# Two PSUM banks for scores used in turn, a new order of work where attention meets the dense feed-forward, and the centring of output rows moved within a batch

## The chip, the cores and the metric

The kernel runs on one NeuronCore of a Trainium2 chip. A core has a matrix engine (PE, with its weight loads shown as PEld), a vector engine (DVE), an activation engine (ACT), GpSimd (POOL) and an engine that issues DMAs (SP). Each runs its own list of instructions in order and waits for the others by semaphores. The metric is the time of one execution in microseconds (us) on the device.

## What is computed

Sixteen sequences of 128 tokens of width 128 go through two layers. All is float32.

```python
x = x + ffn0(attn0(x))     # multi-query attention, 16 heads of 64, relative bias, null key; then layernorm
                           # ffn0: layernorm, 128->512, gelu, layernorm, 512->128, ternary weights
x = x + moe1(attn1(x))     # attention with a given bias per sequence and head, then layernorm
                           # moe1: top 2 of 8 experts, 320 slots each, 128->512, relu, 512->128
# attention, for one sequence b:
xn = ln(x[b]);  q, k, v = xn @ Wq, xn @ Wk, xn @ Wv      # one k and v for all heads
sim = q @ k.T * scale + bias;  sim = where(causal & mask, sim, -big)
out = ln(softmax(sim) @ v @ Wo) * g_out
```

## The kernel before

One batch is one sequence. Both attention layers run a loop over 16 batches, written out for the first and last few and as a hardware loop for those between. The queries of a batch are cut into four units u of 32 query rows. A unit covers all 16 heads, and since attention is causal it needs `WIDTH[u]` = 33, 65, 97, 129 keys.

For each unit PE makes scores in the PSUM tile `psS`, which has two banks: one matmul for each half h of the heads (`scores`, L843 to L857). DVE adds bias and mask, takes the row maximum and writes `sc` (`biased`, L1543 to L1549, four instructions, each of which increments `scores_ready`). ACT takes the exponential (L1255). DVE divides (`divide`, the tile `pn`), PE transposes (`turn_pair`, `turn_probs`), ACT copies to `PT`, PE multiplies by the values (`values_pair` for units 0 and 1, `values` for units 2 and 3), DVE adds the null value and writes `OT` (`outputs`), and PE multiplies by the output weights (`project`). Before the change half h of every unit goes to bank h, so `scores` of unit n waits until `biased` of unit n-1 has ended (`scores_ready` at 4n).

In layer 2 the layernorm of the output rows is spread over later batches on DVE: `out_stats` and `moments`, `variance`, a power of -1/2 on POOL (`output_rstd`), `centre(b-3)` (L1605 to L1611, two instructions, at 128x8 and 128x128, which read two operands from SBUF) and `rescale(b-3)` (L1615). In the kernel before `centre` stands in unit 0 of batch b, behind `divide(B-1, 3)` and ahead of `input_norm(1, b+2)` (tile `xn`, L1498), and `rescale` in unit 1. POOL adds bias and mask for the next batch (`mask_bias`, L630, four instructions each batch) once `output_rstd` is done.

The dense feed-forward stands between the layers. Its 16 tiles are four quads g. PE transposes a quad (`f_turn`), multiplies up (`f_up`, four blocks j), ACT takes the gelu and squares (`f_gelu`, `f_square`), POOL sums squares (`f_squares`), PE multiplies down (`f_down`, 16 tiles), DVE reads the sums and updates the rows X (`f_read`, `f_update`) and takes the statistics of the new rows (`f_input_stats`), whose power POOL takes (`f_input_rstd`). The first seam is where layer 1 ends: the last `values` and `project` on PE, then `f_turn(0)`, `f_up(0, 0)`, `down_sums` and `gate_fold`. The second is where layer 2 begins: `turn_input(1, 0, 0)` needs `xn` of batch 0, then `project_in(0, 0)`, the last four `f_down`, and the first scores.

## Time and profile before

| | us |
|---|---|
| median of 3 runs | 612.4 (610.82 to 613.22) |
| the profiled execution | 614.04 |
| its span, first to last instruction | 612.3 |

The program is bound by no engine all the way: over the span PE is busy 80%, DVE 71%, ACT 62%, POOL 51%. The mean granted clock of PE is 0.931 of full speed. In the page's 40 slices (15.3 us each) PE is at 9 tenths in most of layer 1 (from about 50 to 215 us), at 7 to 9 in the feed-forward and layer 2 (to about 469 us), at 4, 1 and 9 in the routing and the start of the experts. A view's idle time stands in brackets or behind a bar, with the instruction that ended it. Where an engine is late, the chain of waits that ended last passes through it.

### The profile page before, as it was taken

Reading aid. Unit: us, or ns where it says so; the run is one execution under the profiler, and the core shown is the slowest. Engines: PE = TensorE matmul, PEld = TensorE weight load, DVE = VectorE, ACT = ScalarE, POOL = GpSimd, SP = SyncE. Lnnn points to the kernel's source line nnn. Section 1 sums busy time; section 2 is a strip of 40 time slices with the busy share of each in tenths; the row PEclk is TensorE's granted clock in tenths of the full one; section 3 lists DMA queues with packets and bytes.
Section 4 is the critical chain, followed back from the end, with each engine's and each line's share of the span. In section 5 each row is a group of like instructions: output and inputs, shape, how many; then the busy total and the mean of one; then the engine's idle time right before and its main releaser. Section 6 shows DMA issues by size and latency. Waiting matters only on the chain.

```text
span 612.3 us, 13755 instructions
## 1 busy us (share of the span) xinstructions
PE 491.3 (80%) x3220; PEld 395.2 (65%) x3220; DVE 433.2 (71%) x2148; ACT 377.9 (62%) x1475; POOL 310.9 (51%) x368
## 2 busy tenths in 40 slices
PE   3678999999999877948898998988978419999920
PEld 1456777777777655647787887867756307878720
DVE  4899999999999775554778898899797603343403
ACT  1677898888888655634878778767775003443510
POOL 4576666655656517664433343344755531545560
PEclk9789999999999899978899999999998758999975
DMA  5450028331000000000021120000101021222117
GB/s 171 104 151 19 21 60 140 90 97 54 6 8 6 6 1 1 1 0 8 5 77 40 42 75 4 8 6 10 40 26 36 33 74 31 70 61 74 42 34 210
DMA packets 54696, 29.73 MB, mean 49 GB/s; under 512 B 19884, under 2 KB 51572, under 8 KB 54644
## 3 DMA queue, kind: packets, MB, share of 16 engines
q1 hardware_dynamic: 48900, 22.09, 14.6%
q0 software_dynamic: 2560, 4.90, 2.5%
q10 hardware_dynamic: 3184, 2.16, 1.1%
q8 instruction: 18, 0.29, 0.2%
q14 instruction: 34, 0.28, 0.2%
HBM read 16.13 MB, written 10.90 MB: 44 GB/s over the span
## 4 chain that ended last, share of the span: by engine, by line
PE 45%; DVE 20%; issue 14%; POOL 7%; DMA 5%; ACT 4%; SPq 1%; DVEq 1%; another core or an unknown queue 1%; ACTq 0%; POOLq 0%
PE psS L855 9%; PE psS L1152 5%; DVE sc L1547 5%; PE psA L910 4%; PE psO L891 4%; PE psQ L828 4%; PE psQ L812 3%; PE psQ L1142 3%; PE psT L873 2%; DVE centred L1610 2%; DVE OT L1571 2%; POOL wide_buf L630 2%; PE psA L1142 1%; PE psO L1142 1%; ACT qT L1238 1%
## 5 line engine op out<-in xcount | busy, mean ns | idle before, releaser
L1255 ACT ACTIVATE sc<-sc,negmax 128x97 f32<-128x97 f32 (+3 forms) x512 | 179.0, 354 | 34.0 <-DVE negmax L1547 32.2
L855 PE MATMUL psS<-kk,qT 128*128 128x194 f32 (+3 forms) x512 | 104.7, 327 | 23.9 <-DVE negmax L1547 22.2
L1547 DVE CUSTOM_DVE_ANT_0 sc<-psS,wide_buf 128x97 f32<-128x97 f32 (+3 forms) x512 | 93.6, 238 | 29.6 <-PE psS L855 26.6
L630 POOL TENSOR_TENSOR wide_buf<-bias,mask 128x132 f32<-128x132 f32 (+3 forms) x128 | 109.5, 881 | 9.8 <-DVE negmax L1547 4.2
L855 PEld LDWEIGHTS psS<-kk,qT 128*128 128x128 f32 x512 | 79.0, 195 | 50.3 <-issue 47.5
L1255 ACT ACTIVATION_READ_ACCUMULATOR sc<-sc,negmax 128x1 f32 x512 | 97.4, 190 | 0.0
L577 POOL TENSOR_TENSOR qrn<-qssc,half 128x9 f32<-128x9 f32 (+1 forms) x32 | 55.8, 1745 | 59.1 <-DVE qssc L1533 59.1
L1559 DVE TENSOR_TENSOR pn<-sc,rsum 128x128 f32<-128x128 f32 (+3 forms) x128 | 71.7, 560 | 6.8 <-DVE rsum L1555 0.2
L910 PE MATMUL psA<-Wo,OT 128*128 128x128 f32 (+1 forms) x512 | 65.2, 281 | 1.7 <-DVE OT L1571 1.7
L910 PEld LDWEIGHTS psA<-Wo,OT 128*128 128x128 f32 x512 | 62.1, 195 | 2.5 <-DVE OT L1571 2.5
L1571 DVE TENSOR_SCALAR OT<-psO,cols 128x512 f32<-128x512 f32 x64 | 47.6, 744 | 2.7 <-PE psO L891 1.8
L1268 ACT COPY PT<-psT 96x512 f32<-96x512 f32 x64 | 37.0, 577 | 15.8 <-PE psT L873 9.9
L873 PE MATMUL psT<-ident,pn 128*96 128x128 f32 (+1 forms) x256 | 39.6, 278 | 6.0 <-issue 4.1
L1547 DVE DVE_READ_ACCUMULATOR2_ANT negmax<- 128x1 f32 x512 | 41.6, 81 | 0.4 <-issue 0.2
L748 POOL DMA_INDIRECT choice_rows<-hT,tags x24 | 22.5, 939 | 37.1 <-ACT hT L1398 24.5
L891 PE MATMUL psO<-PT,vp 96*64 96x256 f32 (+1 forms) x256 | 34.8, 390 | 7.9 <-DVE OT L1571 4.3
L873 PEld LDWEIGHTS psT<-ident,pn 128*96 128x96 f32 (+1 forms) x256 | 28.5, 137 | 19.1 <-issue 18.5
L642 POOL DMA_INDIRECT slot_rows<-Y,dest_u x32 | 31.4, 980 | 18.1 <-issue 6.7
L812 PE MATMUL psQ<-Wq,xnT 128*128 128x512 f32 x64 | 36.7, 660 | 1.1
L1238 ACT ACTIVATE qT<-psQ 128x512 f32<-128x512 f32 x64 | 34.6, 586 | 4.5 <-PE psQ L841 4.1
L613 POOL TENSOR_TENSOR vp<-kvs,vnull 128x64 f32<-128x64 f32 x32 | 12.9, 403 | 47.2 <-PE psO L891 47.1
L828 PE MATMUL psQ<-xnT,Wq 128*128 128x128 f32 x256 | 32.9, 284 | 0.0
(298 smaller groups left out, 1004.1 us busy)
## 6 DMA issues: line engine op xcount, KB each, us to landing
slot_rows<-empty SPq DMA_DIRECT2D x2, 1390.0 KB, 9.7
xb<-slot_rows SPq DMA_DIRECT2D x16, 139.0 KB
vp_u<-vp SPq DMA_DIRECT2D x128, 8.0 KB, 1.7
choice_rows<-zero_row SPq DMA_DIRECT2D x8, 256.0 KB, 3.0
wide_buf<-choice_rows SPq DMA_DIRECT2D x8, 256.0 KB, 4.7
vp_u<-vp SPq DMA_DIRECT2D x64, 16.0 KB, 1.8
eW<-in_L_ffn_W SPq DMA_DIRECT2D x4, 256.0 KB, 3.0
gT<-in_L_ffn_W SPq DMA_DIRECT2D x4, 256.0 KB, 3.2
```

What stands on the lines that cost most here:

```text
L577: pool.tensor_tensor(dst, src, half[:, 0:k], ALU.pow).then_inc(done, count)
L630: pool.tensor_tensor(unit_masked(i, u).rearrange("p h e k -> p (h e) k"), unit_bias(layer, u).rearrange("p h e k -> p (h e) k"), mask[laye ...
L812: pe.matmul(psQ[:, h, :], xnT[i][:], Wq[0][:, 512 * h:512 * (h + 1)], start=True, stop=True).then_inc(s["q_psum"], 1)
L828: m = pe.matmul(psQ[:, h, j * P:(j + 1) * P], Wq[1][:, (4 * h + j) * P:(4 * h + j + 1) * P], xnT[i][:], start=True, stop=True)
L855: m = pe.matmul(psS[:, h, 0:2 * w], qT[i][:, h, u].rearrange("p m q -> p (m q)"), kk[i][:, :, 0:w], start=True, stop=True)
L873: m = pe.transpose(psT[0:k, probs_bank(u, i), g * P:(g + 1) * P], pn[u][:, g, :], ident[:])
L891: m = pe.matmul(psO[DH * e:DH * (e + 1), 2 * P * (u - 2):2 * P * (u - 1)], vp[i][0:k, :], PT[u - 1][0:k, :, e, :], start=True, stop=True)
L910: m = pe.matmul(psA[:, Y_AT[layer]:4 * P], OT[i][:, j].rearrange("p u q -> p (u q)"), Wo[layer][:, j, :], start=(j == 0), stop=(j == 7))
L1255: m = act.activation(v, v, ACT.Exp, bias=negmax[:, u, g:g + 1], scale=-1.0, accum_out=psum_row[:, u, g:g + 1])
L1547: dve.tensor_tensor_reduce(sc[u][:, h, e, :], unit_psum(u)[:, h, e, :], unit_masked(i, u)[:, h, e, :], -1.0, -FAR, ALU.add, ALU.min, accum ...
L1559: dve.tensor_tensor(pn[u][:], sc[u][:].rearrange("p h e k -> p (h e) k")[:, :, 1:k + 1], rsum[:, u, :].unsqueeze(2).broadcast_to([P, 4, k] ...
L1571: dve.tensor_scalar(OT[i][:, :, 2 * half_of:2 * half_of + 2, :], v, cols[:, C_VN:C_VN + 1], None, ALU.add).then_inc(s["out_ready"], 1)
```

## The change

It has three parts.

1. `score_bank`: unit 0 and 2 have both halves in bank 0, unit 1 in bank 1. Unit 3, which is too wide for one bank, puts half 0 in bank 1 and half 1 in bank 0. `scores` of unit 1, 2 and half 0 of unit 3 wait only for the unit before the last, and half 1 of unit 3 waits for unit 2. Unit 0 waits as before.
2. The seams. On PE `f_turn(0)` is moved ahead of the last `values`, `f_up(0, 0)` ahead of the last `project`, and the wait for the last gelu behind the transposition for layer 2. On DVE `null_keys` and the two `input_norm` of layer 2 are moved from behind `f_input_stats(2)` to ahead of `f_read(2)`, and `values_in(1, 0, 0)` to behind `f_read(2)`. On POOL `f_input_rstd(2)` is moved behind `mask_bias` and `values_set` of layer 2's batch 0.
3. `centre(b-3)` is moved from unit 0 to unit 2 and `rescale(b-3)` from unit 1 to unit 3.

```diff
+        def score_bank(u, h):
+            w = WIDTH[u]
+            if u == UNITS - 1:
+                return psS[:, 1 - h, 0:2 * w]
+            return psS[:, u % 2, 2 * w * h:2 * w * (h + 1)]
...
-                      (s["scores_ready"], 4 * n))
+                      (s["scores_ready"], 4 * (n - u) if u < 2 else 4 * (n - 1)))
                 for h in range(2):
-                    m = pe.matmul(psS[:, h, 0:2 * w], qT[i][:, h, u].rearrange("p m q -> p (m q)"),
+                    if u == UNITS - 1 and h == 1:
+                        apart(pe, (s["scores_ready"], 4 * n))
+                    m = pe.matmul(score_bank(u, h), qT[i][:, h, u].rearrange("p m q -> p (m q)"),
...
                 if g:
                     f_scale(g - 1)
+                if g and g < QUADS - 1:
                     f_input_rstd(g - 1)
...
             values_set(1, 0, 0)
+            f_input_rstd(QUADS - 2)
             f_scale(QUADS - 1)
...
-            pe.wait_ge(s["f_gelu"], 4 * QUADS)
             pe.wait_ge(s["y_done"], NB)
             turn_input(1, 0, 0)
+            pe.wait_ge(s["f_gelu"], 4 * QUADS)
             project_in(0, 0)
...
-                        if u == 0 and normed_now:
-                            centre(b - 3, 1 - i)
                         if u == 0 and not last and not no(b, NB - 2):
                             input_norm(1, b + 2, i)
+                        if u == 2 and normed_now:
+                            centre(b - 3, 1 - i)
...
-                        if u == 1 and normed_now:
+                        if u == 3 and normed_now:
                             rescale(b - 3, 1 - i)
```

PE at the first seam, before: the last transposition of probabilities (L873), the last `values` (L891) and `project` (L910), then `f_turn(0)` (L1070), `f_up(0, 0)` (L1076) and the two lines of `down_sums`.

```order
L873 MATMUL psT<-ident,pn 128x128 x4
L891 MATMUL psO<-PT,vp 64x256 x4
L910 MATMUL psA<-Wo,OT 128x128 x8
L1070 MATMUL psT<-ident,z 128x128 x4
L1076 MATMUL psQ<-hT,w1T 128x512
L1056 MATMUL psO<-w2g,ones 128x128 x4
L1058 MATMUL psO<-w2T,cols 128x128 x4
```

The same place after; lines of the changed kernel are 6 to 11 higher.

```order
L881 MATMUL psT<-ident,pn 128x128 x4
L1076 MATMUL psT<-ident,z 128x128 x4
L899 MATMUL psO<-PT,vp 64x256 x4
L1082 MATMUL psQ<-hT,w1T 128x512
L918 MATMUL psA<-Wo,OT 128x128 x8
L1062 MATMUL psO<-w2g,ones 128x128 x4
L1064 MATMUL psO<-w2T,cols 128x128 x4
```

The transposition and the first up-product have moved in between `values` and `project`, and `down_sums` now follows `project` directly.

DVE at the second seam, before: the end of `f_read(2)`, then `f_update(2)`, `f_input_stats(2)`, the null keys, `xn` and `kvs` (`values_in`).

```order
L1918 SCALAR_TENSOR_TENSOR zve<-fst,fms 128x4
L1923 TENSOR_SCALAR zs<-zrstd,nwm 128x4
L1926 SCALAR_TENSOR_TENSOR X<-ffo,zs,X 128x128 x4
L1933 BN_STATS stats<-X 128x6 x4
L1936 BN_AGGR mv<-stats 128x2 x4
L1938 TENSOR_SCALAR ve<-mv 128x4
L1455 COPY kk<-cols 64x1 x4
L1498 TENSOR_SCALAR xn<-X,mv,rstd 128x128 x2
L1513 COPY kvs<-psA 128x64
```

The same place after, from the end of `f_input_stats(1)`.

```order
L1949 TENSOR_SCALAR ve<-mv 128x4
L1465 COPY kk<-cols 64x1 x4
L1508 TENSOR_SCALAR xn<-X,mv,rstd 128x128 x2
L1925 COPY fst<-psS 128x2
...
L1929 SCALAR_TENSOR_TENSOR zve<-fst,fms 128x4
L1523 COPY kvs<-psA 128x64
L1934 TENSOR_SCALAR zs<-zrstd,nwm 128x4
L1937 SCALAR_TENSOR_TENSOR X<-ffo,zs,X 128x128 x4
```

`xn` now stands ahead of the reads of quad 2, and `kvs` behind them.

DVE in layer 2's loop, unit 0 to 1, before: `pn` of the last batch's unit 3, the two instructions of `centre`, `xn`, and the first of `biased` of unit 1 (rows named ISA without a tile are waits).

```order
L1559 TENSOR_TENSOR pn<-sc,rsum 128x512
L1607 REGISTER_ALU
L1608 ISA
L1608 SCALAR_TENSOR_TENSOR centred<-gate_sum,o_mv,Y 128x8
L1610 ISA
L1610 SCALAR_TENSOR_TENSOR centred<-Y,o_mv,g_out 128x128
L1498 ISA x2
L1498 TENSOR_SCALAR xn<-X,mv,rstd 128x128
L351 ISA
L1547 ISA sc,negmax<-psS,wide_buf 128x65
```

The same place after, and the new place of `centre` in unit 2.

```order
L1570 TENSOR_TENSOR pn<-sc,rsum 128x512
L1508 ISA x2
L1508 TENSOR_SCALAR xn<-X,mv,rstd 128x128
L355 ISA
L1557 ISA sc,negmax<-psS,wide_buf 128x65
...
L1608 BN_AGGR o_mv<-o_st 128x2
L1619 ISA
L1619 SCALAR_TENSOR_TENSOR centred<-gate_sum,o_mv,Y 128x8
L1621 ISA
L1621 SCALAR_TENSOR_TENSOR centred<-Y,o_mv,g_out 128x128
L355 REGISTER_ALU
L1557 ISA sc,negmax<-psS,wide_buf 128x129
```

`xn` now follows `pn` directly, and `centre` stands ahead of `biased` of unit 3. ACT's order is the same in both kernels.

## Rows read from the trace of the kernel before

**Rows 1.** Windows: stretch, length; busy PE, PEld, DVE, ACT, POOL; granted clock; DMA.

```profile
322.37:390.77 68.40, 62.41 (x469) 54.50 (x469) 58.78 (x306) 54.75 (x241) 26.33 (x36) 1.00 0.14 37
390.77:468.90 78.13, 66.67 (x483) 56.19 (x484) 68.28 (x384) 56.59 (x253) 38.54 (x48) 0.98 0.07 20
468.90:504.77 35.87, 11.40 (x94) 9.53 (x91) 15.20 (x80) 4.29 (x15) 17.40 (x20) 0.70 0.19 54
```

**Rows 2.** Groups of PE, layer 1, 50:214.9: count, busy, mean ns, idle before.

```profile
L855 PE MATMUL psS<-kk,qT 128*128 128x66 f32 (+3 forms) x224 | 45.1, 323 | 4.6 <-DVE negmax L1547 3.0
```

**Rows 3.** Groups of PE, six steady batches of layer 2, 322.3:390.7.

```profile
L855 PE MATMUL psS<-kk,qT 128*128 128x194 f32 (+3 forms) x96 | 18.9, 318 | 2.0 <-DVE negmax L1547 2.0
...
L891 PE MATMUL psO<-PT,vp 96*64 96x256 f32 (+1 forms) x48 | 6.5, 388 | 2.4 <-DVE OT L1571 2.4
```

**Rows 4.** Groups of PE, the last batches of layer 2, 390.77:468.9.

```profile
L855 PE MATMUL psS<-kk,qT 128*128 128x194 f32 (+3 forms) x104 | 21.4, 328 | 7.7 <-DVE negmax L1547 7.6
...
L891 PE MATMUL psO<-PT,vp 96*64 96x256 f32 (+1 forms) x56 | 7.6, 389 | 1.6 <-DVE OT L1571 1.6
```

**Rows 5.** Timeline of DVE in one steady batch: start, us, instruction.

```profile
341.21 0.95 DVE L1559 TENSOR_TENSOR pn<-sc,rsum 128x512 f32<-128x512 f32 x1
342.09 0.86 DVE L1608 SCALAR_TENSOR_TENSOR centred<-gate_sum,o_mv,Y 128x8 f32<-128x8 f32 x1
342.87 1.30 DVE L1610 SCALAR_TENSOR_TENSOR centred<-Y,o_mv,g_out 128x128 f32<-128x128 f32 x1
344.09 0.34 DVE L1498 TENSOR_SCALAR xn<-X,mv,rstd 128x128 f32 x1
```

**Rows 6.** Timeline of POOL, the same batch.

```profile
340.56 3.46 POOL L630 TENSOR_TENSOR wide_buf<-bias,mask 128x132 f32<-128x132 f32 x4
```

**Rows 7.** Timeline of PE, the same batch; in brackets the idle time before it.

```profile
345.15 0.90 PE L855 MATMUL psS<-kk,qT 128*128 128x194 f32 x4 [0.40 <-DVE negmax L1547]
```

**Rows 8.** Groups of DVE, `centre` behind layer 2's loop, 470:490.

```profile
L1610 DVE SCALAR_TENSOR_TENSOR centred<-Y,o_mv,g_out 128x128 f32<-128x128 f32 x3 | 1.0, 345 | 0.0
...
L1608 DVE SCALAR_TENSOR_TENSOR centred<-gate_sum,o_mv,Y 128x8 f32<-128x8 f32 x3 | 0.7, 224 | 2.9 <-POOL o_rs L577 2.9
```

**Rows 9.** Groups of DVE, five steady batches, 339:396.7, widest and narrowest `biased`.

```profile
L1547 DVE CUSTOM_DVE_ANT_0 sc<-psS,wide_buf 128x129 f32<-128x129 f32 x20 | 4.6, 288 | 3.6 <-PE psS L855 3.6
...
L1547 DVE CUSTOM_DVE_ANT_0 sc<-psS,wide_buf 128x33 f32<-128x33 f32 x20 | 2.8, 193 | 2.4 <-PE psS L855 2.4
```

**Rows 10.** Timeline of DVE, batch 0 of layer 2.

```profile
286.74 1.25 DVE L1498 TENSOR_SCALAR xn<-X,mv,rstd 128x128 f32<-128x128 f32 x1
```

**Rows 11.** Timeline of PE at the first seam.

```profile
222.81 1.09 PE L891 MATMUL psO<-PT,vp 96*64 96x256 f32 x8 [0.88 <-issue]
224.74 2.05 PE L910 MATMUL psA<-Wo,OT 128*128 128x128 f32 x16 [0.85 <-DVE OT L1571]
...
228.10 1.13 PE L1076 MATMUL psQ<-hT,w1T 128*128 128x512 f32 x2 [0.87 <-ACT hT L1351]
229.06 1.05 PE L1056 MATMUL psO<-w2g,ones 128*128 128x128 f32 x8
```

**Rows 12.** Timeline of PE at the second seam.

```profile
273.13 0.44 PE L801 MATMUL psA<-ident,xn 128*128 128x128 f32 x1 [7.21 <-issue]
...
275.05 3.48 PE L828 MATMUL psQ<-xnT,Wq 128*128 128x128 f32 x16
...
278.48 1.06 PE L1085 MATMUL psS<-w2g,gT 128*128 128x129 f32 x8
...
282.86 0.41 PE L819 MATMUL psA<-Wkv,xnT 128*128 128x64 f32 x2
...
283.39 1.95 PE L828 MATMUL psQ<-xnT,Wq 128*128 128x128 f32 x16
285.18 0.56 PE L855 MATMUL psS<-kk,qT 128*128 128x66 f32 x4
```

**Rows 13.** Timeline of POOL at the second seam.

```profile
273.01 3.00 POOL L630 TENSOR_TENSOR wide_buf<-bias,mask 128x132 f32<-128x132 f32 x4
```

More of the change, by code:

```diff
@@ L989, in attention_first @@
                 turn_probs(NB - 1, 3, 1)
-                values(NB - 1, 1)
-                project(0, NB - 1, 1, False)
             def attention_second():
@@ L1089, in f_down @@
                           stop=True).then_inc(s["f_o_psum"], 1)
+            pe.wait_ge(s["probsT_ready"], 3 * NB - 1)
+            f_turn(0)
+            values(NB - 1, 1)
             pe.wait_ge(s["g_WoT"], 2)
-            pe.wait_ge(s["probsT_ready"], 3 * NB)
-            f_turn(0)
+            f_up(0, 0)
+            project(0, NB - 1, 1, False)
             for g in range(QUADS):
                 for j in range(FB):
-                    f_up(g, j)
+                    if g or j:
+                        f_up(g, j)
                     if g == 0 and j == 0:
@@ L1546, in biased @@
                     h, e = g // 2, g % 2
-                    dve.tensor_tensor_reduce(sc[u][:, h, e, :], unit_psum(u)[:, h, e, :], unit_masked(i, u)[:, h, e, :],
+                    dve.tensor_tensor_reduce(sc[u][:, h, e, :], score_bank(u, h)[:, e * WIDTH[u]:(e + 1) * WIDTH[u]],
+                                             unit_masked(i, u)[:, h, e, :],
                                              -1.0, -FAR, ALU.add, ALU.min,
@@ L1942, in _ @@
                     f_norm_in(g + 2)
+                if g == QUADS - 2:
+                    null_keys(cols[:, C_NK:C_NK + 1])
+                    dve.wait_ge(s["x_rstd"], 1)
+                    input_norm(1, 0, 0)
+                    input_norm(1, 1, 1)
                 f_read(g)
+                if g == QUADS - 2:
+                    values_in(1, 0, 0)
                 f_update(g)
                 f_input_stats(g)
-            null_keys(cols[:, C_NK:C_NK + 1])
-            dve.wait_ge(s["x_rstd"], 1)
-            input_norm(1, 0, 0)
-            input_norm(1, 1, 1)
-            values_in(1, 0, 0)
             f_read(QUADS - 1)
-            dve.wait_ge(s["x_rstd"], QUADS - 1)
+            dve.wait_ge(s["x_rstd"], QUADS - 2)
             attention_second()
```

2 lines of the change are left out of this document (removed).

## Prediction

> **What bounds the kernel now.** I read the stretches first, then what PE waits for in each, then single batches. The windows show that PE is nearly full in the steady part of layer 2, 62.4 of 68.4 us, with 6.0 us idle in six batches, and less full in its last batches, 66.7 of 78.1 [rows 1]. So in attention a gain is at most PE's idle time. The groups of PE say who ends that idle time. In layer 1 the scores matmuls have 4.6 us of idle ahead of them from 50 to 215 us, about 14 batches [rows 2]. In the six steady batches of layer 2 it is 2.0 us ahead of scores and 2.4 ahead of `values`, both ended by DVE [rows 3], and in the last batches 7.7 and 1.6 [rows 4]. At the seams PE idles for another reason: it stands at one instruction whose operand comes late while later work would be ready. The largest such hole is 7.21 us, ahead of layer 2's first transposition [rows 12].
>
> Why DVE is late in layer 2 is seen in one batch. `pn` of unit 3 takes 0.95 us, then the two instructions of `centre` take 0.86 and 1.30, and `xn` 0.34 [rows 5]. The same two take 0.22 and 0.35 behind the loop [rows 8]. In the loop they run while POOL's four adds run, from 340.56 to 344.02 [rows 6], and the second ends just behind the last add. So (0.86 - 0.22) + (1.30 - 0.35) = 1.6 us of each batch is DVE standing behind POOL. It makes `biased` of unit 1 late, for which PE's scores of unit 2 wait 0.40 [rows 7], and then `OT`, for which `values` waits 2.4 / 6 = 0.40 [rows 3].
>
> **Part 1 and 3 in layer 2.** With alternating banks the scores of unit 2 wait for unit 0, which has long been read, so their 0.40 goes whether DVE is faster or not. With `centre` gone from unit 0, `xn` is next behind `pn`, and POOL's adds still run. An `xn` that starts under POOL's adds is held too: in batch 0 it took 1.25 us in place of 0.34 [rows 5, 10]. So the stall is not removed whole. `centre`'s first instruction shows what one such wait costs there, 0.64, since it was let in when POOL's third add ended. I give `xn` that wait and drop the second one, so DVE reaches unit 1 some 1.2 us earlier, at 343.1 in place of 344.3. Then `pn` of unit 0 may stand behind the fourth add until 344.1. `OT` still ends about 1.0 us sooner, and PE, which comes 0.4 sooner, finds it. So of the 0.73 us per batch ahead of scores and `values` nearly all goes: 4.2 us in six batches, and 0.7 in the batch before them, which is built alike. What comes late next is the transposition of unit 3 behind `pn`, which the change does not touch; it is part of the 6.0 - 4.4 = 1.6 us of idle that stay.
>
> The moved instructions cost at their new places 0.22 + 0.35 in unit 2 and 0.28 in unit 3. In the steady batches DVE waits there for PE: in five batches 3.6 us ahead of the widest `biased` (unit 3) and 2.4 ahead of the narrowest (unit 0), 0.7 and 0.5 a batch [rows 9], and POOL's adds are over by then. Behind them stand `biased` of unit 3 and of unit 0. I cost both at nothing; without that cover they would be 0.3 us a batch, some 3 us in all.
>
> In the last batches DVE has the routing too and is itself the bound. The bounds for these 78 us are what six steady batches give, 4.4, and all idle ahead of scores and `values`, 9.3 [rows 4]. Unit 0's scores keep their old wait, and part of the 7.7 is theirs. But each stall taken from DVE counts there in full. I take 6.0. Layer 2 sums to 4.2 + 0.7 + 6.0 = 10.9 us, bounds 3 and 14.
>
> The Trainium skill, SBUF — State Buffer, section "Who interferes with whom", says that a DVE instruction with two SBUF inputs, or a one-input `tensor_scalar` in a two-port mode, shares its second port with GpSimd, and that whoever starts first holds it for a whole instruction. It speaks against part 3 so far as `xn` is a `tensor_scalar` and inherits the place; with the rule taken as one add per wait the sum is as above, and with `xn` missing the gap between two adds it is rival A. The trace agrees that `xn` can be held, 1.25 against 0.34 us.
>
> **Part 1 in layer 1.** Of the 4.6 us ahead of scores 3.0 are waits long enough to be given to DVE, and 1.6 are short ones [rows 2]. Half 0 of unit 3 no longer waits for unit 2, and half 1, which does, has half 0's own matmuls ahead of it as cover. The larger waits are DVE being late as a whole, and a bank more lets PE run ahead by one unit. Bounds 0 and 4.6; I take 2.0, the short ones and a little. The added wait in unit 3 has behind it all of PE, but it is for what the old one waited for.
>
> **The first seam.** PE waits 0.88 for `values`, 0.85 for `project` and 0.87 for `f_up(0, 0)`, the last for ACT's copy of `hT` [rows 11]. Now the four transpositions of `f_turn(0)` run in the first hole, and ACT's copy runs under `values` (1.09). `f_up(0, 0)` takes 229.06 - 228.10 = 1.0 and fills the second hole. `values` ends at 222.81 + 1.09 = 223.9 as before, `f_up` at 224.95, which is when `project` starts in place of 224.74, and with its 2.05 us `down_sums` starts at 227.0 in place of 229.06 [rows 11]. Everything behind it waits for it: DVE's `c2`, POOL's adds to X, and the fold of the gate. That is 2.1 us; bounds 1 (if POOL's and DVE's work behind it holds part back) and 2.5.
>
> **The second seam.** PE ended its last ready work at 273.13 - 7.21 = 265.92 [rows 12]. The `xn` of batches 0 and 1 are rows of quad 0, final long before, so DVE can write them ahead of `f_read(2)`. That puts six short instructions ahead of reads, of which the last waits for PE's work that ends at 265.92 anyway, so they cost nothing. From there: the transposition, ACT's copy and the first matmuls of `project_in`, 275.05 - 273.13 = 1.9 at the low clock, for which I take 1.4; the sixteen of L828, 1.95; the four `f_down`, 282.86 - 278.48 = 4.4; `project_in` of batch 1, 285.18 - 282.86 = 2.3; in all 10.05 us [rows 12]. The first scores come at 276.0 in place of 285.18: 9.2 us. The clock: the hole was followed by 3.48 us for sixteen matmuls that take 1.95 otherwise [rows 12], the 1.2 GHz level in place of 2.4. Without the hole I take the high level; if it drops all the same, 2 us are lost.
>
> Two things stand against it. POOL now does `mask_bias` of batch 0 some 4 us earlier, beside DVE's `f_update(2)`, four instructions with two SBUF operands each. They may be held for most of POOL's 3.00 us of adds [rows 13], which puts `f_read(3)`'s end about where PE comes to the first scores. And POOL's power of quad 2 now stands ahead of `f_scale(3)`, so the adds for batch 1 start about 1 us later against the first scores than before. Bounds 4 and 11, value 9.2, since PE's own work is nearest to the end.
>
> **Sum.** 10.9 + 2.0 + 2.1 + 9.2 = 24.2 us. The profiled execution took 614.04, which gives 589.8. The median of the runs shown is 1.6 lower, so **588.2**. Routing and experts (from 469 us on) are unchanged in order and shift as a whole.
>
> **Rivals.** A: *`xn` takes over the stall.* If `xn` always waits for POOL's last add, as in batch 0 (1.25 us) [rows 10], DVE's chain is shorter only by 0.3 us. The scores of unit 2 go early, but `values` waits for the same `OT`; layer 2 gives 3 and the time is 596. For it speaks that row, against it that `pn` and the first `centre` instruction each got in between two adds [rows 5]. B: *the second seam gives half.* POOL's order or the low clock holds the first batch back: 4 to 5 us less, 593. For it speaks that batches 0 and 1 depend on DVE, POOL and PE at once; against it PE's count above [rows 12]. C, *slower:* PE is granted 1.2 GHz in attention. The change moves idle time, and layer 2 at the low level would run near 1.8 times as long for its 62.4 us of PE work in 68.4 [rows 1]. It costs 0.45 us for each us spent there, so it outweighs 24 us from a spell of some 55 us on, and 3 us more make it slower: 616. Against it: the clock is 1.00 in that stretch, and even behind layer 2, where PE is busy 11.4 of 35.9 us, the mean is 0.70, some 21 us at the low level [rows 1]. D: *the waits are only renamed*, the bound in attention being a loop through DVE and ACT: only the seams gain, 601. Against it is that PE is 91% busy in the steady batches.
>
> **How the numbers follow.** The forecast has 0.68, A 0.12, B 0.12, D 0.03, C 0.02, and 0.03 is left for something that cancels all. The terms' own bounds give 582 to 594 for the forecast's case. The range of 582 to 598 takes in A and B. A measurement of this kernel tells about 0.5% (3 us) from no change. Faster by more holds in the forecast, A, B and D: 0.95; within 0.5% 0.03; slower 0.02.
>
> **What would show it.** After the change PE's groups should show under 1 us ahead of scores and under 0.5 ahead of `values` in six steady batches, and a batch should take 10.6 us in place of 11.4. `xn` in unit 0 should take about 1 us, `centre` 0.22 and 0.35. The first scores of layer 2 should start some 13 us earlier, near 272, and layer 1 end 2 us earlier. `xn` at 1.3 us in every batch with `OT` still ending PE's idle would be A; a hole of 4 us or more around the first scores would be B; a clock under 0.9 in layer 2 would be C. The prediction is wrong as a whole if a batch of layer 2 still takes 11.2 us.

## The result, and the profile after the change

The changed kernel takes 587.8 us (median of 4 runs, 587.1 to 592.0); the kernel before, run beside it, 611.6. The ratio is 0.962, 95% interval 0.958 to 0.966. Two later sets of runs of the same kernel gave 588.5 and 588.3 us, with ratios of 0.962 and 0.961. The forecast was 588.2.

The profiled executions differ by more, 612.3 and 586.0, 26.3 us. The table splits them by what can be read in a timeline of PE: the start of the first scores matmul of a batch. "Again" is the same changed kernel in the profiles of the two later sets.

| stretch (us) | before | after | again | again |
|---|---|---|---|---|
| layer 1, batch 2 to 15 | 154.1 | 152.9 | 152.9 | 152.9 |
| batch 15 to layer 2's first scores (both seams) | 79.1 | 67.2 | 66.2 | 66.3 |
| layer 2, batches 0 to 2 | 31.9 | 32.7 | 33.4 | 33.7 |
| layer 2, batches 3 to 9 | 79.7 | 73.1 | 73.1 | 73.1 |
| layer 2, batches 10 to 14 | 61.2 | 56.6 | 57.7 | 57.3 |
| batch 15 to the end | 154.3 | 151.9 | 151.3 | 151.7 |

The seam's 67.2 and 66.2 differ by a spell at the lower level of the clock (granted 0.50, 1.2 GHz). In the first profile of the changed kernel it lies from 205.0 to 208.4, at the end of layer 1, and PE is busy throughout it; the other two have none there. The kernel before has one at the same place, from 206.6 to 210.0, so its 79.1 is best set against 67.2.

Of the last row's 2.4 to 3.0 us, 1.7 to 2.1 lie behind the last matmul, where nothing was changed. That tail is 26.4 us in the profile of before, 24.3 to 24.7 in the three of the changed kernel and 23.3 to 24.4 in the four that carry one part each. So some 2 us of the 26.3 belong to the tail of the one profile that there is of the kernel before, which fits that the medians differ by less than the spans.

The groups of PE's instructions in the changed kernel say where the idle time went. Columns: line, operation, tiles, count, busy us, mean ns, idle us just before. First layer 1, 50:213, then the steady batches of layer 2, 309:377, then the last ones, 377.5:444. They answer to [rows 2], [rows 3] and [rows 4]. The line ahead of them is the kernel before, layer 1, 50:215.

```profile
L873 PE MATMUL psT<-ident,pn 128*96 128x128 f32 (+1 forms) x112 | 17.5, 280 | 1.4 <-issue 0.3
```

```profile
L863 PE MATMUL psS<-kk,qT 128*128 128x66 f32 (+3 forms) x224 | 45.1, 323 | 1.6 <-DVE negmax L1557 1.6
...
L881 PE MATMUL psT<-ident,pn 128*96 128x128 f32 (+1 forms) x112 | 17.5, 280 | 3.3 <-issue 3.1
```

```profile
L863 PE MATMUL psS<-kk,qT 128*128 128x194 f32 (+3 forms) x104 | 20.0, 314 | 0.0
L899 PE MATMUL psO<-PT,vp 96*64 96x256 f32 (+1 forms) x56 | 7.6, 392 | 0.0
L881 PE MATMUL psT<-ident,pn 128*96 128x128 f32 (+1 forms) x48 | 7.4, 276 | 2.1 <-issue 1.9
```

```profile
L863 PE MATMUL psS<-kk,qT 128*128 128x66 f32 (+3 forms) x95 | 18.6, 315 | 2.6 <-DVE negmax L1557 2.6
...
L899 PE MATMUL psO<-PT,vp 96*64 96x256 f32 (+1 forms) x48 | 6.5, 390 | 1.9 <-DVE OT L1582 1.9
```

In the steady batches the idle time ahead of scores (2.0) and of `values` (2.4) is gone. What is left stands ahead of the transposition of unit 3. In layer 1 the 4.6 us ahead of scores became 1.6, but the group of transpositions, 1.4 before, now has 3.3: of the 3.0 us that are gone in one place 1.9 stand in another.

The windows of the changed kernel, for [rows 1]: length, busy PE, PEld, DVE, ACT, POOL, granted clock, share of DMA. One steady batch has no idle time of PE at all, and batch 0 has a great deal.

```profile
304.45:314.58 10.13, 10.13 (x81) 8.91 (x80) 8.77 (x52) 9.04 (x40) 4.50 (x6) 1.00 0.21 60
304.40:377.40 73.00, 70.88 (x548) 62.31 (x548) 63.32 (x356) 63.26 (x281) 31.99 (x42) 1.00 0.16 43
```

The same for batch 0, the changed kernel and then the kernel before:

```profile
271.71:284.26 12.55, 7.83 (x43) 6.83 (x41) 9.00 (x58) 9.79 (x41) 8.04 (x10) 0.73 0.05 10
```

```profile
285.18:296.90 11.72, 8.42 (x43) 7.19 (x41) 8.80 (x54) 8.85 (x39) 6.87 (x9) 0.71 0.03 7
```

DVE in one steady batch, for [rows 5], and POOL there, for [rows 6] (start, duration, instruction), then the groups of DVE in five such batches, 325:377.4:

```profile
347.47 0.86 DVE L1570 TENSOR_TENSOR pn<-sc,rsum 128x512 f32<-128x512 f32 x1
348.25 0.92 DVE L1508 TENSOR_SCALAR xn<-X,mv,rstd 128x128 f32 x1
...
346.74 3.44 POOL L634 TENSOR_TENSOR wide_buf<-bias,mask 128x132 f32<-128x132 f32 x4
```

```profile
L1508 DVE TENSOR_SCALAR xn<-X,mv,rstd 128x128 f32 x5 | 4.8, 967 | 0.0
...
L1621 DVE SCALAR_TENSOR_TENSOR centred<-Y,o_mv,g_out 128x128 f32<-128x128 f32 x5 | 1.7, 341 | 0.0
...
L1619 DVE SCALAR_TENSOR_TENSOR centred<-gate_sum,o_mv,Y 128x8 f32<-128x8 f32 x5 | 1.0, 195 | 0.0
```

`centre` takes 0.20 and 0.34 at its new place, where POOL is idle, and `xn` has inherited the held place: 0.97 in place of 0.34.

PE's timelines at the two seams answer to [rows 11] and [rows 12]:

```profile
221.19 1.09 PE L899 MATMUL psO<-PT,vp 96*64 96x256 f32 x8 [0.44 <-issue]
222.21 1.12 PE L1082 MATMUL psQ<-hT,w1T 128*128 128x512 f32 x2
223.17 2.00 PE L918 MATMUL psA<-Wo,OT 128*128 128x128 f32 x16
225.01 1.06 PE L1062 MATMUL psO<-w2g,ones 128*128 128x128 f32 x8
```

```profile
261.74 0.31 PE L807 MATMUL psA<-ident,xn 128*128 128x128 f32 x1
...
263.12 1.95 PE L834 MATMUL psQ<-xnT,Wq 128*128 128x128 f32 x16
...
271.71 0.56 PE L863 MATMUL psS<-kk,qT 128*128 128x66 f32 x4
```

From `values` to `down_sums` it was 6.25 us (222.81 to 229.06) and is 3.82. At the second seam the hole of 7.21 us is gone and the first scores start at 271.71. But behind them, in batch 0, there is a new one:

```profile
279.07 1.20 PE L863 MATMUL psS<-kk,qT 128*128 128x258 f32 x2 [3.99 <-DVE negmax L1557]
```

### The profile page after: what moved, and what is told of

The parts are those of the page before. It is cut to its first block, busy times and chain, and to the rows that moved or that the text cites. A ratio compares the mean times of both kernels' runs of the same rounds, so it can differ in the third digit from the quotient of the medians.

```text
span 586.0 us, 13781 instructions
## 1 busy us (share of the span) xinstructions
PE 483.6 (83%) x3220; PEld 390.9 (67%) x3220; DVE 426.4 (73%) x2148; ACT 377.5 (64%) x1475; POOL 312.0 (53%) x368
## 3 DMA queue, kind: packets, MB, share of 16 engines
q1 hardware_dynamic: 48900, 22.09, 15.1%
## 4 chain that ended last, share of the span: by engine, by line
PE 59%; DVE 12%; issue 11%; POOL 6%; ACT 4%; DMA 4%; SPq 1%; another core or an unknown queue 1%; DVEq 0%; ACTq 0%; POOLq 0%
PE psS L863 10%; PE psA L918 7%; PE psS L1162 5%; PE psQ L834 4%; PE psT L881 4%; PE psO L899 4%; PE psQ L818 4%; PE psQ L1152 3%; PE psO L889 2%; DVE sc L1557 2%; PE psO L890 2%; DMA slot_rows<-Y,dest_u 1%; ACT qT L1248 1%; PE psO L1152 1%; PE psA L1152 1%
## 5 line engine op out<-in xcount | busy, mean ns | idle before, releaser
L863 PE MATMUL psS<-kk,qT 128*128 128x194 f32 (+3 forms) x512 | 102.7, 322 | 11.6 <-DVE negmax L1557 11.6
L581 POOL TENSOR_TENSOR qrn<-qssc,half 128x9 f32<-128x9 f32 (+1 forms) x32 | 55.9, 1748 | 57.8 <-DVE qssc L1543 57.7
L881 PE MATMUL psT<-ident,pn 128*96 128x128 f32 (+1 forms) x256 | 39.6, 278 | 11.0 <-issue 10.6
L617 POOL TENSOR_TENSOR vp<-kvs,vnull 128x64 f32<-128x64 f32 x32 | 14.1, 440 | 40.3 <-PE psO L899 40.2
L1979 DVE TENSOR_SCALAR hm<-psQ,cols 128x320 f32<-128x320 f32 x16 | 8.8, 551 | 32.4 <-PE psQ L1152 32.4
```

The source lines that it names most:

```text
L581: pool.tensor_tensor(dst, src, half[:, 0:k], ALU.pow).then_inc(done, count)
L863: m = pe.matmul(score_bank(u, h), qT[i][:, h, u].rearrange("p m q -> p (m q)"), kk[i][:, :, 0:w], start=True, stop=True)
L881: m = pe.transpose(psT[0:k, probs_bank(u, i), g * P:(g + 1) * P], pn[u][:, g, :], ident[:])
```

## The experiments

### One part at a time

Four kernels, each the kernel before with one part of the change: alternating banks with the split of unit 3 (its two halves in different banks), the order at both seams, `centre` and `rescale` two units later, and the second seam alone. The first and the third edit are these; the seams are the pieces of the diff shown ahead of the prediction.

```
-                      (s["scores_ready"], 4 * n))
+                      (s["scores_ready"], 4 * (n - u) if u < 2 else 4 * (n - 1)))
...
+                    if u == UNITS - 1 and h == 1:
+                        apart(pe, (s["scores_ready"], 4 * n))
```

```
-                        if u == 0 and normed_now:
+                        if u == 2 and normed_now:
                             centre(b - 3, 1 - i)
...
-                        if u == 1 and normed_now:
+                        if u == 3 and normed_now:
                             rescale(b - 3, 1 - i)
```

Part 1 alone:

> The kernel before with part 1 alone (alternating banks). Theory: in layer 2 PE's idle time ahead of scores is only where DVE's lateness shows first, so with the bank free PE does the scores of unit 2 at once and then waits for the same OT ahead of values. Six steady batches stay at about 68 us, the idle ahead of scores falls from 2.0 to near 0 and that ahead of values rises from 2.4 to 4 or more; the gain is layer 1's, 2 to 3 us in all: 608.5 to 610. Rival: the shared banks cost PE in layer 2 as the rows say, 2.0 us in six batches and part of 7.7 in the last ones; then the gain is 7 to 9 us, 603 to 605.

Part 2 alone:

> The kernel before with part 2 alone (both seams). Theory: 2.1 us at the first seam and 9.2 at the second, of which about 1 is given back in layer 2's batch 0, where POOL's adds and DVE's update of quad 3 now stand closer to the first scores: 600.5 to 602. Rival: the seams only shift the point at which DVE and POOL are full, and part is lost again in the first batches: 604 or more.

Part 3 alone:

> The kernel before with part 3 alone (centring in unit 2). Theory: DVE's stall behind POOL's adds is what makes PE wait both ahead of scores and ahead of values, so this part alone gives nearly all of layer 2's gain: 9.5 to 12 us, 600 to 602; a steady batch takes 10.5 to 10.6 us in place of 11.4, xn about 0.9 us, centre 0.2 and 0.35. Rival: half of it needs the free bank: 4 to 6 us, 606 to 608.

The second seam alone:

> The kernel before with the second seam's order alone. Theory: the seams add up, the second gives 8 to 9.5 us, 602 to 603.5, and the first what is between this and both seams, about 2. Rival: PE's clock falls to 1.2 GHz behind the seam all the same or batch 0 waits longer, and the second seam gives 6 us or less, 605.5.

Measured, beside the kernel before at 611.7 us, with the stretches of the profiles:

| | banks | both seams | second seam | centring |
|---|---|---|---|---|
| median, us | 607.7 | 600.8 | 603.1 | 602.4 |
| ratio | 0.994 (0.991 to 0.997) | 0.985 (0.980 to 0.991) | 0.988 (0.983 to 0.994) | 0.987 (0.981 to 0.994) |
| layer 1, batch 2 to 15 | 152.9 | 154.0 | 154.0 | 154.1 |
| both seams | 77.9 | 66.2 | 68.6 | 79.0 |
| layer 2, batches 0 to 2 | 31.3 | 33.9 | 33.5 | 31.9 |
| batches 3 to 9 | 79.1 | 79.7 | 79.7 | 72.7 |
| batches 10 to 14 | 60.1 | 61.1 | 60.3 | 59.4 |

All four medians lie in the theory's ranges or within 1 us of them. The ratios' gains sum to 3.3%, 20.4 us with the two seams counted once, against 3.8% of the whole change; the intervals are wide enough for the parts to be additive.

The stretches are sharper than the medians, since most of them repeat to 0.1 us. The 6.6 us of layer 2's steady batches are wholly those of part 3: with it alone they take 72.7, with the banks alone 79.1, with both 73.1. The groups of PE in the steady batches show what the banks do there. First the banks alone (318.5:386.5), then the centring alone (321.5:383.5):

```profile
L861 PE MATMUL psS<-kk,qT 128*128 128x194 f32 (+3 forms) x98 | 18.7, 311 | 0.0
...
L897 PE MATMUL psO<-PT,vp 96*64 96x256 f32 (+1 forms) x48 | 6.5, 388 | 4.6 <-DVE OT L1578 4.6
```

```profile
L855 PE MATMUL psS<-kk,qT 128*128 128x194 f32 (+3 forms) x96 | 18.7, 316 | 0.0
...
L891 PE MATMUL psO<-PT,vp 96*64 96x256 f32 (+1 forms) x48 | 6.5, 392 | 0.0
```

With the banks alone the wait ahead of scores is gone, and the one ahead of `values`, 2.4 in [rows 3], is 4.6: PE reaches the same late `OT` earlier. With the centring alone both waits are gone, and no bank is needed. The seams are worth 79.1 - 66.2 = 12.9, of which 1.2 is not theirs: with the banks alone, which touch no seam, the same stretch is 77.9. Of this 1.0 is the clock and not the banks; the other 0.2 stand behind layer 2's first transposition and were not followed up. The profiles of the kernel before and of the centring alone have the spell at 1.2 GHz at the end of layer 1 (206.6 to 210.0 and 206.3 to 209.7), and from the first scores of batch 15 to the end of the last `values` both take 17.8 us. The profiles of the banks, of both seams and of the second seam have none there and take 16.8. Among these three the second seam gives 77.9 - 68.6 = 9.2 and the first 68.6 - 66.2 = 2.4. Both kernels with the new second seam then lose 1.6 to 2.0 us in batches 0 to 2.

### What in part 1 helps layer 1

The changed kernel with one change in a wait: the first half of unit 3 waits for unit 2 too, so the banks alternate but the split covers nothing.

```
-                      (s["scores_ready"], 4 * (n - u) if u < 2 else 4 * (n - 1)))
+                      (s["scores_ready"], 4 * (n - u) if u < 2 else (4 * (n - 1) if u == 2 else 4 * n)))
```

> The changed kernel, but in unit 3 the first half of the scores waits for unit 2 as the second half does. It prices the split inside part 1. My theory: of the 1.6 us that layer 1 gained most is the wait of unit 2, which now looks two units back, and little is the split: layer 1, from its first to its last batch, stays within 0.4 us of the changed kernel's (180.0 in its profile), the time within 1 us of it (587 to 589), and layer 2's steady batches stay at 10.4 us. Rival (the gain of layer 1 is the split, since its matmuls cover the wait of unit 3): layer 1 is 1 to 1.6 us longer and the time 589 to 590.

It took 591.1 us, ratio 0.966 (0.963 to 0.969). Layer 1 from batch 2 to 15 takes 154.1 us, what it took before the change; so here the rival was right and my theory wrong. The groups of PE in layer 1, 50:213:

```profile
L863 PE MATMUL psS<-kk,qT 128*128 128x66 f32 (+3 forms) x222 | 43.2, 315 | 3.4 <-DVE negmax L1557 1.8
...
L881 PE MATMUL psT<-ident,pn 128*96 128x128 f32 (+1 forms) x112 | 17.2, 276 | 4.5 <-issue 4.4
```

The alternation as such gives layer 1 nothing. The gain of 1.2 us there is the split, which gives PE half of unit 3's matmuls while it would wait. Layer 2's steady batches seem to lose by the split: 72.75 us without it, 73.05 with it, and 72.71 with no bank changed at all. But all of that is one batch, the sixth of the seven, which takes 11.06 us with the split and 10.32 without; the six others together are 0.4 us shorter with it. In that batch `pn` of unit 3 starts 0.1 us later against POOL's adds. DVE and POOL, first the changed kernel, then the one without the split:

```profile
357.96 1.43 DVE L1570 TENSOR_TENSOR pn<-sc,rsum 128x512 f32<-128x512 f32 x1
...
356.94 3.44 POOL L634 TENSOR_TENSOR wide_buf<-bias,mask 128x132 f32<-128x132 f32 x4
```

```profile
358.89 0.69 DVE L1570 TENSOR_TENSOR pn<-sc,rsum 128x512 f32<-128x512 f32 x1
...
357.96 3.46 POOL L634 TENSOR_TENSOR wide_buf<-bias,mask 128x132 f32<-128x132 f32 x4
```

It starts 1.02 us behind the first add in one and 0.93 in the other, and takes 0.74 us more; PE's stop ahead of the transposition that needs it is 0.93 us in place of 0.19. So this stall does cost time, unlike that of `xn`, which comes next.

### Whether the stall that `xn` took over costs time

```
-                        if u == 0 and not last and not no(b, NB - 2):
+                        if u == 1 and not last and not no(b, NB - 2):
                             input_norm(1, b + 2, i)
```

> The changed kernel, with input_norm (DVE's xn) moved from unit 0 of a batch to unit 1 in layer 2. My theory: in the changed kernel xn has inherited the place behind pn of unit 3 and is held there by POOL's adds (0.97 us for work of 0.34), but PE is full in the steady batches (idle 2.1 us in seven, all of it ahead of a transposition), so DVE's lost time costs nothing: the time stays within 1 us of the changed kernel's 587.8, the steady batch stays at 10.4 us, xn falls to 0.35 to 0.5 us, and what comes next behind pn (biased of unit 1) starts some 0.6 us earlier. Only in the last batches, where DVE has the routing too, up to 1 us may come. Rival (the inherited stall still costs, case A of the prediction): 3 to 5 us less, 583 to 585, with a steady batch of 10.1 us.

It took 589.5 us, ratio 0.961 (0.959 to 0.964); the changed kernel in the same set 588.5, 0.962. The group of DVE in five steady batches, 325:377.4, and the window of seven batches:

```profile
L1570 DVE TENSOR_TENSOR pn<-sc,rsum 128x128 f32<-128x128 f32 x5 | 4.0, 797 | 0.7
...
L1508 DVE TENSOR_SCALAR xn<-X,mv,rstd 128x128 f32 x5 | 1.7, 331 | 0.0
```

```profile
304.40:377.40 73.00, 70.88 (x549) 62.34 (x548) 61.87 (x357) 63.28 (x280) 31.99 (x42) 1.00 0.16 43
```

`xn` falls from 0.97 to 0.33 us, and the seven batches take 73.02 us in place of 73.05, with PE busy 70.88 us in the same 73.00 as before. The place of `xn` costs nothing there, as the theory has it. But the stall isn't gone: `pn` of unit 0, the next instruction with two operands in SBUF, now takes 0.80 us in place of 0.34, and DVE's busy time over the seven batches falls by 1.45 us only, 0.2 a batch. So the run shows that 0.2 us less of DVE and an earlier `biased` of unit 1 bring nothing; it doesn't show what a DVE without any stall would bring. That stalls still cost time is seen elsewhere: of PE's 2.1 us of idle time in these seven batches 1.8 stand ahead of the transposition of unit 3 in two batches, where `pn` of unit 3 was held to 1.13 and 1.43 us.

### The hole in batch 0

Two steps of DVE in batch 0 go one unit later each (the first edit); then that together with `xn` in unit 1; then an Exp of one column ahead of layer 2 (the second edit), alone and with the two others. The changed kernel ran beside them in both sets.

```
-                        if first and u == 1:
+                        if first and u == 2:
                             f_update(QUADS - 1)
-                        if first and u == 2:
+                        if first and u == 3:
                             f_input_stats(QUADS - 1)
```

```
             queries(1, 0, 0)
+            act.activation(warm[:], cols[:, C_GIN1:C_GIN1 + 1], ACT.Exp, scale=0.0)
             attention_second()
```

`f_update(3)` later:

> The changed kernel, with two steps of DVE in batch 0 of layer 2 each put one unit later: f_update(3) from unit 1 to unit 2, f_input_stats(3) from unit 2 to unit 3. My theory: PE's hole of 3.99 us ahead of the second half of unit 3's scores in that batch is made by DVE, whose biased of unit 2 stands behind f_update(3), 0.28 + 1.67 us; it starts 1.9 us earlier now and the hole becomes 2.0 to 2.2 us. Without a spell at 1.2 GHz behind it batch 0 takes 9.9 to 10.6 us in place of 12.55; with one it takes 10.6 to 11. The time is 1.5 to 2.7 us less than the changed kernel's, 585 to 586.3. Rival (the hole is the latency of the chain through ACT's exponentials when the pipeline fills, and f_update only stands in it): no change, 587 to 588, with the hole still over 3.3 us.

That and `xn` in unit 1:

> The changed kernel, with input_norm in unit 1 and f_update(3) and f_input_stats(3) of batch 0 each one unit later. My theory: the sum of the two runs before, which is the second one's alone: 585 to 586.3, first batch of layer 2 at 10 to 11 us. Rival: with xn in unit 1 of batch 0 that unit's chain becomes longer again by 0.4 us, and 0.4 us of the gain goes.

The changed kernel beside them:

> The changed kernel itself, beside its variants on the same chip. Every theory expects 587 to 588.5 us and, in its profile, 12 to 13 us for batch 0 of layer 2 with a hole of 3 to 4 us ahead of the second half of unit 3's scores. If the spell at 1.2 GHz in that batch is an accident of this one trace, it is absent here.

The early Exp:

> The changed kernel, with one more instruction of ACT: an Exp of one column into a tile that nobody reads, behind queries(1, 0, 0), ahead of layer 2. There ACT is idle for 5.8 us, and in batch 0 its first exponential is preceded by a table load of 1.28 us. My theory: batch 0 is a chain that fills (scores, biased, exponentials, divide, next scores), and PE's hole in it is the length of that chain, of which the table load is 1.28 us; f_update(3) only stands in it behind. With the load done early the first exponentials start 1.3 us sooner and the hole of 3.99 us becomes 2.7 to 3.0; batch 0 is 1.0 to 1.3 us shorter, and the time 586 to 587.3. Rival (POOL's adds then hold f_update(3) by as much, or the hole is DVE's own work): under 0.4 us in batch 0, no change.

All three edits:

> The kernel with input_norm in unit 1 and f_update(3) and f_input_stats(3) one unit later (e7), with the early Exp too. My theory: e7's hole of 2.23 us in batch 0 is the wait for the first exponentials and falls to about 1.0; batch 0 takes 10.0 to 10.4 us in place of 11.5, and the time is 1.0 to 1.3 us under e7's, 3 to 3.5 under the changed kernel's: 584 to 585.5. Rival (the clock falls to its lower level in batch 0 all the same and stretches PE's own work there): batch 0 stays over 10.8 us and half of the gain goes.

The changed kernel beside these:

> The changed kernel itself, beside its variants on the same chip. All theories expect 587.5 to 588.5 us, with the table load of 1.28 us ahead of ACT's first exponentials of layer 2, and batch 0 of layer 2 at 12.5 to 13.2 us.

| | median, us | ratio | batch 0 | batches 0 to 2 | batches 10 to 14 |
|---|---|---|---|---|---|
| changed kernel (three profiles) | 587.8, 588.5, 588.3 | 0.962, 0.962, 0.961 | 12.5, 13.2, 13.3 | 32.7, 33.4, 33.7 | 56.6, 57.7, 57.3 |
| update later | 590.6 | 0.963 (0.961 to 0.966) | 12.4 | 33.3 | 57.7 |
| update later, `xn` in unit 1 | 586.3 | 0.957 (0.954 to 0.960) | 11.5 | 31.7 | 56.5 |
| early Exp | 589.5 | 0.963 (0.961 to 0.966) | 11.7 | 31.9 | 59.6 |
| all three | 588.6 | 0.962 (0.958 to 0.965) | 9.1 | 30.8 | 60.1 |

The update alone does nothing for the time. In PE's timeline the hole of 3.99 falls to 2.08, as expected, but a second one opens:

```profile
276.48 0.67 PE L863 MATMUL psS<-kk,qT 128*128 128x258 f32 x2 [2.08 <-DVE negmax L1557]
...
279.01 0.69 PE L825 MATMUL psA<-Wkv,xnT 128*128 128x64 f32 x2 [1.30 <-ACT xnT L1224]
```

PE then waits for ACT, which makes `xnT` only behind the exponentials of units 1 and 2. So the rival was nearer: the hole is a chain through DVE and ACT that fills, and `f_update(3)` only stands in it. What that chain contains is seen on ACT. First the kernel before, then the changed one, and then the one with the early Exp:

```profile
284.65 1.28 ACT L1255 ACT_TABLE_LOAD   x1
```

```profile
272.36 0.26 ACT L1258 COPY kk<-psA 64x128 f32<-64x128 f32 x1 [5.81 <-issue]
...
272.91 1.28 ACT L1265 ACT_TABLE_LOAD   x1
```

```profile
265.64 1.28 ACT L1388 ACT_TABLE_LOAD   x1
266.94 0.20 ACT L1388 ACTIVATE warm<-cols 128x1 f32<-128x1 f32 x1
```

Before the change the load started 0.5 us ahead of layer 2's first scores and was done when the first `biased` began (285.91 in its timeline). Now it starts 1.2 us behind the first scores. The order on the queues is the old one: ahead of the load stand ACT's copies of `kk` for batch 1, which wait until DVE has copied `kvs`, and that copy stands behind `f_read(3)`. But `kvs` was copied at 283.80, 1.4 us ahead of the first scores, and is now copied at 272.06, 0.35 behind them, as PE's part of the seam became shorter and DVE's did not. With the load at 265.6 batch 0 takes 11.7 us, 0.8 to 1.6 less. But the hole is 3.79 still, against the 2.7 to 3.0 expected. The first exponentials do start as early as before the change, 1.26 us behind the first scores in place of 2.50, and `f_update(3)` starts 1.1 us sooner, yet ends only 0.2 sooner. DVE and POOL in the kernel with the early Exp:

```profile
274.23 1.09 DVE L1936 TENSOR_SCALAR zs<-zrstd,nwm 128x4 f32<-128x4 f32 x1
...
272.26 3.04 POOL L635 TENSOR_TENSOR wide_buf<-bias,mask 128x132 f32<-128x132 f32 x4
```

`zs` takes 1.09 us under POOL's adds and 0.28 behind them in the changed kernel. That is this run's rival: POOL's adds hold `f_update(3)` by about as much as the load did. They start 1.5 us behind the first scores in every kernel with the new second seam, and 0.27 ahead of them in every kernel without it. What batch 0 gained beyond 0.2 us goes with PE's rate: PE is busy 7.2 us in place of 7.8 to 8.5, and the granted clock is 0.85 in that batch against 0.73 to 0.76. Whether the early load has to do with the clock, no run shows. With all three edits batch 0 takes 9.1 us at full clock; against the kernel without the early Exp PE is busy 2.1 us less there and idle 0.4 us less, so most of that gain too goes with the clock. The windows of batch 0, the early Exp first, then all three:

```profile
270.78:282.50 11.72, 7.20 (x43) 6.19 (x42) 10.06 (x58) 8.52 (x40) 8.10 (x10) 0.85 0.05 11
```

```profile
270.38:279.47 9.09, 6.26 (x42) 4.80 (x41) 8.24 (x48) 7.24 (x35) 6.41 (x10) 1.00 0.06 13
```

That is better than I had expected of batch 0, and the next batch gives 1.5 of it back (11.3 us in place of 9.8). Of batches 0 to 2 as a whole 2 to 3 us are won, yet the time is the changed kernel's. In the profile the rest was lost in batches 10 to 14. One instruction of DVE shows how. First DVE and POOL with all three edits, then the same place in the kernel without the early Exp:

```profile
411.19 2.91 DVE L1572 TENSOR_TENSOR pn<-sc,rsum 128x512 f32<-128x512 f32 x1
...
410.57 2.98 POOL L635 TENSOR_TENSOR wide_buf<-bias,mask 128x132 f32<-128x132 f32 x4
```

```profile
412.42 0.98 DVE L1570 TENSOR_TENSOR pn<-sc,rsum 128x512 f32<-128x512 f32 x1
...
411.81 3.43 POOL L634 TENSOR_TENSOR wide_buf<-bias,mask 128x132 f32<-128x132 f32 x4
```

And what PE saw of each:

```profile
414.20 1.09 PE L882 MATMUL psT<-ident,pn 128*128 128x128 f32 x4 [2.84 <-issue]
```

```profile
413.50 0.63 PE L881 MATMUL psT<-ident,pn 128*128 128x128 f32 x4 [0.17 <-issue]
```

`pn` starts 0.6 us behind POOL's first add in both. In one it is let in (0.98 us, and POOL's adds take 3.43 in all), in the other it is held until POOL has finished (2.91 us, and the adds take 2.98, the time that they have for themselves). PE's hole is 2.7 us longer, a spell at 1.2 GHz follows it (413.8 to 417.2), and the batch takes 14.4 us in place of 10.7. One such event cancels an edit of this size. I can't say from these runs how often it happens in one kernel or the other: in the fourteen profiles it stands once in the kernel with all three edits and once in the one with both seams alone (3.01 us), and in no other. The profile with the early Exp alone lost 2 to 3 us in the same batches without it, in holes of 1.2, 0.8, 0.5 and 0.7 us. The first and the last of them stand behind a `pn` of unit 3 that took 1.27 and 1.46 us, against 0.98 and 0.70 in the changed kernel; the other two I did not separate.

Whether a variant beats the changed kernel is not settled. The best median is 586.3, with the update and `xn` moved. Its interval (0.954 to 0.960) overlaps those of the changed kernel, which reach from 0.958 to 0.966, and the kernel that contains it and the early Exp shows no gain at all.

## Why the prediction was right, and where it was not

**The total.** 24.2 us were summed and 23.9 measured between the medians. Part of that is luck: layer 2's steady batches gave more than their term, while layer 1 and the last batches gave less, and batch 0 gave some back that the sum had at nothing. The range is no product of the terms either: added up as they stand, their bounds give 581 to 604, and not 582 to 594.

**Layer 2's steady batches: right in kind, too small, and credited to the wrong part.** I gave 0.70 us a batch and it is 0.95; a batch takes 10.4 us, not 10.6. The waits ahead of scores and `values` went to nothing, as said. Two steps of the sum failed. One is "their 0.40 goes whether DVE is faster or not": it goes with the banks, but to the next wait, for `OT`, and the batch is shorter by 0.08 only. I had the same fact in hand for case D (a wait that is only renamed) and applied it to the change as a whole instead of to this part. The other is the size. I took PE's idle time as all that there was to gain. Over seven batches PE's holes fell from 6.9 to 2.1 us, by 4.8, while the stretch fell by 6.65. The missing 1.9 us are time that the profile counts as busy. A batch of the kernel before with three stops, a batch of the changed kernel with one:

```profile
351.19:362.61 11.42, 10.45 (x81) 9.13 (x80) 9.82 (x52) 9.14 (x41) 4.30 (x6) 1.00 0.19 52
```

```profile
356.24:367.30 11.06, 10.13 (x80) 8.91 (x79) 9.71 (x53) 9.04 (x40) 4.57 (x6) 1.00 0.03 6
```

It goes by where the stop stands and not by how many there are. The second batch has a stop of 0.93 us ahead of the transposition, and its 10.13 us are what the batch without any stop has. With the banks alone a batch whose one long stop is ahead of `values` (1.03 us, 336.09 to 347.38) is busy 10.21. So a stop ahead of the transposition hides nothing, one ahead of `values` 0.08 us, and of the 0.32 between 10.45 and 10.13 some 0.24 is left for the one ahead of scores. The rows give a reason for part of that, as an estimate: ahead of these scores stand matmuls of `project`, which start 0.12 us apart in a row while a single one is recorded with 0.28, so 0.16 us of a stop behind them counts as busy.

**`xn`.** It takes 0.97 (about 1 was said), and moving it away shows that its place costs nothing in the steady batches. Case A, that the stall goes on costing 8 us, fell. The Trainium skill, SBUF — State Buffer, section "Who interferes with whom", says that whoever issues first gets the shared pair for the whole instruction. The prediction read that as one add per wait, and the trace agrees in all but two cases: a `pn` of unit 3 that is held ends 0.55 to 0.6 us behind the end of one add, and POOL's next add is the longer one (the counts are in the last section). The two don't fit: `pn` at 411.19 came 0.62 us behind the first add and stood through the rest of POOL's four.

**Layer 1.** 2.0 us were given, 1.2 came from batch 2 to 15. I ascribed it to the short waits of unit 2; it is the cover of unit 3, which I had named and not counted on.

**The first seam.** 2.1 was given; it is 2.4, the same by two kernels that differ in it alone.

**The second seam.** 9.2 us to the first scores, as given, and they start at 271.7, where "near 272" was said. The sixteen matmuls of L834 take 1.95 us at the high level, as taken; they took 3.48 before. POOL's `mask_bias` did hold `f_update(2)`, 3.08 us in place of 1.14, and that fitted in. Here is the one step left out: the working ends at the first scores. Behind them PE needs the `biased` and the exponentials of batch 0, and these moved later against the scores: the first exponentials from 1.26 to 2.50 us behind them, the end of `f_update(3)` from 5.53 to 6.50. I had put the end of `f_read(3)` "about where PE comes to the first scores", which is where it is, and did not ask what stands behind it: `kvs`, the copies of `kk` and the table load. The other half was in the working and priced at nothing: POOL's adds for batch 1 "about 1 us later against the first scores", which is 1.7 (from 0.27 ahead of them to 1.47 behind). The early Exp takes away the first delay and leaves the second, and the hole stays. PE's idle time in batch 0 rose by 1.4 us, from 3.3 to 4.7 in all three profiles, and batches 0 to 2 gave back 0.8 to 1.7 us. Case B named a hole of 4 us or more around the first scores as its sign, and it is there, 3.99; its price was far smaller than B's 4 to 5 us, for batch 0 had holes before too, 1.24, 1.06 and 1.01 us.

**The last batches.** 6.0 was given, for a stretch that ran on into batch 15, and 3.5 to 4.6 measured in batches 10 to 14; from batch 15 to the last matmul 0.6 to 0.8 came besides. The banks alone gave 1.1 in batches 10 to 14, the centring alone 1.8. The second may be too low a price: in its profile batch 11 takes 15.1 us against 13.0 to 13.3 in the others, behind a stop of 1.73 us and with a spell at 1.2 GHz from 407.7 to 411.1. What the two parts give together beyond what each gives alone stays open, since batch 13 alone takes 10.3 to 14.4 us in these profiles.

**The clock.** Case C did not occur: 1.00 in the steady batches. In batch 0 of the changed kernel the granted clock fell to the lower level (1.2 GHz) in all three of its profiles, in the one shown from 276.6 to 283.5 us, while PE stood in the hole that ended at 279.07. But the kernel before has a spell in its batch 0 too, from 288.5 to 295.3 us, with a mean of 0.71 over the batch against 0.73, so this is no part of what batch 0 gave back. The 2 us that the sum named for the clock were for the low level ahead of the first scores, and that did not come.

## What to carry to other kernels

A second buffer takes away the wait for that buffer and nothing else: ask first which wait comes next on the same instruction stream, and whether the same late engine ends it. Follow a seam's working to the first steady batch, not to its first instruction, with the table loads and the copies that stand ahead of them on each queue. Look where PE's stops stand and compare its busy time too, for a stop can hide up to 0.24 us more than its idle time shows. Before a gain of a few tenths is credited to an edit, look whether the edit has only moved an instruction across a boundary of another engine's work: 0.1 us did that here and cost 0.74. And read the granted clock of a stretch in both profiles before it explains a difference.

## What was not expected of the hardware

How long `pn` of unit 3 (128x512, two operands in SBUF) is held follows from when it starts against POOL's four adds, nearly always. It takes 0.69 us when POOL is idle. In layer 2 of the fourteen profiles 168 of them start within 2.5 us of the first add:

| start behind the first add, us | count | what follows |
|---|---|---|
| 0.07 | 3 | ends at 0.97 |
| 0.40 to 0.81 | 95 | ends at 1.58 to 1.61, so takes 0.78 to 1.19 |
| 0.98 to 1.44 | 30 | ends at 2.43 to 2.46, so takes 1.00 to 1.46 |
| 0.27 to 0.34, 0.89 to 0.99, 1.82 | 37 | takes 0.69 to 0.70 |
| 2.43 | 1 | takes 1.12 |
| 0.52 and 0.62 | 2 | take 3.01 and 2.91 |

The adds themselves start at 0, 0.38, 1.00 and 1.86 when nothing stands between them; the one behind a `pn` that was let in takes longer, the third for instance 1.34 in place of 0.89. So the two engines take turns by whole instructions, and a start at 1.0 us decides between 0.69 and 1.43. Why two of the 168 were passed over twice more was not found; others that started at the same 0.52 and 0.61 us took 1.07 and 0.98. A small instruction is held as well: `centre`'s of 128x8 took 0.86 under the adds, 0.20 without them.

The load of ACT's table took 1.28 us, and the next instruction of ACT began as it ended (265.64 and 266.94 above). The Trainium skill, ScalarE: Activation LUTs, section "What ACT_TABLE_LOAD costs", gives 1283 ns for the load and 1380 more for a drain; the trace agrees with the first and shows none of the second. An instruction whose result nobody reads brings the load forward; the kernel with it took 589.5 us against 588.3 beside it, a difference within the intervals.

The same program shows the lower clock at different places, and what a spell costs depends on where it lies. Of the three profiles of the changed kernel one has a spell from 205.0 to 208.4, in which PE is busy throughout, and its seam takes 67.2 us. One has a spell from 233.6 to 237.0, and its seam takes 66.3, against 66.2 in the third, which has none. In batch 0 the granted clock was 0.73 in the changed kernel, 0.70 with the update and `xn` moved, 0.85 with the early Exp and 1.00 with all three edits. PE's idle time there was 4.7, 3.2, 4.5 and 2.8 us in the same order, so the clock doesn't go by the idle time of the batch alone.
